# Splitting the fourth row group of the last convolution pass into three and two tiles, and moving the counts of the first search among the sums

## The reference, cut to what matters

```
m   = segment_sum(xt[src], dst) * Binv          # passes 0 and 2 (counts)
out = segment_sum(m[dst], src) * Dinv + b       # passes 1 and 3 (counts transposed)
h = prelu(hconv(x, W1, b1)); h = hconv(h, W2, b2) + x; x = x + prelu(h)
weights = layernorm(x) @ wr + br                # router
sel = the 1561 rows with the largest weights    # top-k
x[sel] += gelu(ln(x)[sel] @ w1 + b1) @ w2 + b2, times the weight of the row
```

## Time and profile before

| | |
|---|---|
| median of three runs | 1784.41 us |
| the three runs | 1784.41, 1785.26, 1777.81 us |
| the profiled execution | 1781.41 us |
| its span in the trace | 1779.7 us |
| PE busy | 1597.2 us (90%), 11957 matmuls |
| DVE busy | 1070.2 us (60%) |
| ACT busy | 1090.4 us (61%) |
| mean granted PE clock | 0.953 of full |

### The profile page before, as it was taken

The page is one execution under the profiler, slowest core; times in us unless marked ns, Lnnn a source line. Parts: engine busy times, 40 slices in busy tenths (PEclk is TensorE's granted clock), DMA queues, the critical chain, the costliest instruction groups (busy, mean ns, idle before and its releaser), DMA issues. The chain is left out here.

```text
span 1779.7 us, 35628 instructions
## 1 busy us (share of the span) xinstructions
PE 1597.2 (90%) x11957; PEld 1405.4 (79%) x11957; DVE 1070.2 (60%) x1890; ACT 1090.4 (61%) x1999; POOL 80.9 (5%) x116
## 2 busy tenths in 40 slices
PE   5777677699999999998999799999999999998697
PEld 4666666599999999996666599987789998776465
DVE  5598889579999999997455411214241122577671
ACT  2377778688888888884334466565665555565121
POOL 3000000000000000002000100000000000021213
PEclk9888888699999999998999899999999999999699
DMA  7325555256031212203000144445554444575211
GB/s 204 91 70 159 159 166 155 86 145 134 16 87 26 70 48 57 54 1 87 1 0 0 41 125 122 123 110 136 136 128 124 123 123 108 139 181 139 62 31 52
DMA packets 134299, 170.02 MB, mean 96 GB/s; under 512 B 17104, under 2 KB 125829, under 8 KB 134178
## 3 DMA queue, kind: packets, MB, share of 16 engines
q1 hardware_dynamic: 124268, 155.61, 33.3%
q0 software_dynamic: 6368, 9.36, 2.1%
q10 hardware_dynamic: 3542, 3.46, 0.8%
HBM read 114.58 MB, written 53.76 MB: 95 GB/s over the span
## 5 line engine op out<-in xcount | busy, mean ns | idle before, releaser
L1611 PE MATMUL ps_sets<-arena,kinds_mem 125*125 125x195 bf16 (+1 forms) x2500 | 447.4, 247 | 24.8 <-DVE kinds_mem L1370 16.7
L1354 ACT ACTIVATE kinds_mem<-ed_rows,es_mask 125x625 bf16<-125x625 f32 x500 | 367.2, 810 | 59.6 <-PE ps_sets L1617 31.3
L1617 PE MATMUL ps_sets<-arena,kinds_mem 125*125 125x195 bf16 (+1 forms) x2300 | 397.0, 248 | 0.0
L1611 PEld LDWEIGHTS ps_sets<-arena,kinds_mem 125*125 125x125 bf16 x2500 | 342.6, 137 | 31.8 <-DVE kinds_mem L1370 23.6
L2779 ACT ACTIVATE onewide<-ring 125x625 fp32r (+1 forms) x350 | 239.7, 721 | 180.4 <-PE oneps L2508 106.7
L1617 PEld LDWEIGHTS ps_sets<-arena,kinds_mem 125*125 125x125 bf16 x2300 | 308.3, 134 | 0.0
L2480 PE MATMUL oneps<-onewide,parts_a 125*128 125x376 f32 (+1 forms) x2000 | 294.3, 309 | 9.4 <-DVEq L2567 7.7
L2480 PEld LDWEIGHTS oneps<-onewide,parts_a 125*128 125x128 f32 x2000 | 292.3, 190 | 10.5 <-DVEq L2565 8.1
L2508 PE MATMUL oneps<-oneparts_b,onewide 125*125 125x512 f32 x1125 | 263.7, 395 | 0.0
L2508 PEld LDWEIGHTS oneps<-oneparts_b,onewide 125*125 125x125 f32 x1125 | 207.6, 185 | 54.7 <-DVE onefull L2639 2.1
L1362 DVE TENSOR_TENSOR kinds_mem<-kinds_mem,blk 125x2500 bf16<-125x2500 bf16 x120 | 182.4, 1520 | 33.9 <-ACT kinds_mem L1354 28.6
(11 more groups left out here) (457 smaller groups left out, 1838.5 us busy)
## 6 DMA issues: line engine op xcount, KB each, us to landing
ring<-counts SPq DMA_DIRECT2D x50, 683.6 KB
ring<-countsT SPq DMA_DIRECT2D x45, 683.6 KB
countsT<-kinds_mem SPq DMA_DIRECT2D x25, 683.6 KB
blk<-counts SPq DMA_DIRECT2D x20, 546.9 KB
counts<-blk SPq DMA_DIRECT2D x3, 3418.0 KB
counts<-kinds_mem SPq DMA_DIRECT2D x2, 3418.0 KB
ed_rows<-ed_dram SPq DMA_DIRECT2D x16, 273.4 KB
ring<-counts SPq DMA_DIRECT2D x50, 79.3 KB
```

The lines of the kernel that those rows point to most:

```text
L1354: return k.nc.scalar.activation(kinds_of(k)[:, slot, 0, :], k.ed_b[:, h, :], ACT.Relu, scale=MASK_SCALE, bias=k.es_mask[:, t, h:h + 1])
L1611: t_.matmul(out[0], kind[0], z[0], start=(t == 0), stop=False)
L1617: last = t_.matmul(out[1], kind[1], z[1], start=False, stop=(t == T - 1))
```

## The change

The fourth row group (i = 3) of pass 3 is taken out of the loops over the groups and is done as the last one is: tiles 0, 1, 2 over all t, then tiles 3, 4. Its chunks of counts are fetched twice as often, 125 x 375 and then 125 x 250 elements a t. DVE takes its banks part by part, finishes the rows of a part and does the dot products of that part at once; `x_done` is posted behind the rows of the second part, ahead of their dot products, and `row_weights` is cut into `row_dots` and `row_scales`. ACT takes the roots of group 2 ahead of t = 20 of group 3's first part, and those of group 3 ahead of t = 15 of group 4's first part. All eight counts of the search stand among the sums of the last group, the first at t = 14 of its first part instead of t = 20.

```diff
-def row_weights(dve, root_done, n, v, k, std, i, junk):
-    tiles = slice(i * U, (i + 1) * U)
+def row_dots(v, k, i, junk, some=range(U)):
+    tiles = slice(i * U + some[0], i * U + some[-1] + 1)
     v.tensor_copy(k.stat[:, tiles, 0], k.MV[:, tiles, 0])
     v.drain()
-    for u in range(U):
+    for u in some:
         t = i * U + u
         v.scalar_tensor_tensor(out=junk[:, u, :], in0=k.X[:, t, :], scalar=k.stat[:, t, 0:1], in1=k.wr_b[:, :],
                                op0=ALU.subtract, op1=ALU.mult, accum_out=k.dot[:, t:t + 1])
+    v.drain()
+
+def row_scales(dve, root_done, n, v, k, std, i):
+    tiles = slice(i * U, (i + 1) * U)
     dve.wait_ge(root_done, n)
     v.reciprocal(k.stat[:, tiles, 1], std[:, tiles])
...
-    COUNTS_AT = ((0, 20), (0, 24), (1, 5), (1, 10), (1, 15), (1, 20)) if len(counts) == 1 else ()
+    COUNTS_AT = ((0, 14), (0, 18), (0, 22), (0, 24), (1, 5), (1, 11), (1, 17), (1, 22)) if len(counts) == 1 else ()
+    def chunk_of(i, part):
+        return Q_LAST - 1 + (i - U + 2) * len(LAST) + part
...
-                for part in range(len(LAST)):
-                    for s in range(NS):
-                        last_counts_in(part, s)
+                for i in range(U - 2, U):
+                    for part in range(len(LAST)):
+                        for s in range(NS):
+                            last_counts_in(i, part, s)
...
-                            if (part, t) in COUNTS_AT:
+                            if i == U - 1 and (part, t) in COUNTS_AT:
                                 choice_counts(pe, t_, k, s1, COUNTS_AT.index((part, t)))
...
-                    with pe.Fori(1, U if c == 0 else U - 1) as i:
+                    with pe.Fori(1, U if c == 0 else U - 2) as i:
                         sums(2 * c + 1, i, {})
                 pe.wait_ge(z_free, 3 * 2 * U + 3)
-                last_sums()
+                last_sums(U - 2)
+                last_sums(U - 1)
...
-                def rows_out(n, i):
-                    v.tensor_scalar(tmp[:, :, :], full[:, :, :], 0.0, slope[:, 0:1], ALU.min, ALU.mult)
+                def rows_out(n, i, some=range(U)):
+                    part = slice(some[0], some[-1] + 1)
+                    v.tensor_scalar(tmp[:, part, :], full[:, part, :], 0.0, slope[:, 0:1], ALU.min, ALU.mult)
...
-                    means_out(3, i)
-                    rows_out(3, i)
-                    v.nop().then_inc(x_done, 1)
+                    for some in LAST if i == U - 2 else (range(U),):
+                        means_out(3, i, some)
+                        rows_out(3, i, some)
+                        if i == U - 2:
+                            if some[-1] == U - 1:
+                                v.nop().then_inc(x_done, 1)
+                            row_dots(v, k, i, full, some)
+                    if i < U - 2:
+                        v.nop().then_inc(x_done, 1)
...
-                weights(U - 2)
+                row_scales(dve, root_done, U - 1, v, k, std, U - 2)
+                v.nop().then_inc(weights_done, 1)
...
-                for i in range(1, U - 1):
+                for i in range(1, U - 2):
                     widen(3, i, {3 * U + 2: lambda: roots(i - 1)})
-                for part, some in enumerate(LAST):
-                    c0, c1 = some[0] * P, (some[-1] + 1) * P
-                    for t in range(TB):
-                        s = t // U
-                        if part == 0 and t == 3 * U + 4:
-                            roots(U - 2)
...
+                for i, root_at in ((U - 2, 4 * U), (U - 1, 3 * U)):
+                    for part, some in enumerate(LAST):
+                        c0, c1 = some[0] * P, (some[-1] + 1) * P
+                        chunk = chunk_of(i, part)
+                        for t in range(TB):
+                            s = t // U
+                            if part == 0 and t == root_at:
+                                roots(i - 1)
...
```

More of the change, by code:

```diff
@@ L2333, in convolutions_phase, with sums_before @@
     Q_LAST = 4 * U - 1
-    COUNTS_AT = ((0, 20), (0, 24), (1, 5), (1, 10), (1, 15), (1, 20)) if len(counts) == 1 else ()
+    COUNTS_AT = ((0, 14), (0, 18), (0, 22), (0, 24), (1, 5), (1, 11), (1, 17), (1, 22)) if len(counts) == 1 else ()
+    def chunk_of(i, part):
+        return Q_LAST - 1 + (i - U + 2) * len(LAST) + part
+    def sums_before(i):
+        return (U - 1) * (Q_LAST - 1) + (i - U + 2) * (U - len(LAST))
     with scope(nc, later) as (sb, pb, sem):
@@ L2385, in counts_in, with last_counts_in @@
                         sp.dma_start(ring[lo_:hi_, slot, :, :].rearrange("p a t d -> p (a t) d"), src[lo_:hi_]).then_inc(c_in[s % U], 16)
-                def last_counts_in(part, s):
+                def last_counts_in(i, part, s):
                     c0, c1 = LAST[part][0] * P, (LAST[part][-1] + 1) * P
-                    src = STEPS[3][s // U][(s % U) * QB:(s % U + 1) * QB, (U - 1) * QB + c0:(U - 1) * QB + c1].rearrange("(t p) d -> p t d", p=P)
-                    chunk = NS * (Q_LAST + part) + s
+                    src = STEPS[3][s // U][(s % U) * QB:(s % U + 1) * QB, i * QB + c0:i * QB + c1].rearrange("(t p) d -> p t d", p=P)
+                    chunk = NS * chunk_of(i, part) + s
                     sp.wait_ge(wide_done, U * chunk + U)
@@ L2514, in sums, with last_sums @@
                             after[s]()
-                def last_sums():
+                def last_sums(i):
                     for part, some in enumerate(LAST):
                         for t in range(TB):
-                            pe.wait_ge(wide_done, TB * (Q_LAST + part) + t + 1 + RB * U)
+                            pe.wait_ge(wide_done, TB * chunk_of(i, part) + t + 1 + RB * U)
                             for kk in some:
                                 if t == 0:
-                                    pe.wait_ge(c_out, U * Q_LAST + kk + 1)
+                                    pe.wait_ge(c_out, U * (3 * U + i) + kk + 1)
                                 last = t_.matmul(ps[0:P, kk, :], wide[:, t % RF, kk * P:(kk + 1) * P], ROWS[3][:, t % T, 0:2 * F],
@@ L2621, in means_out @@
                     for kk in some:
-                        if n == 3 and i == U - 1:
+                        if n == 3 and isinstance(i, int) and i >= U - 2:
                             part = LAST.index(tuple(some))
                             if kk == some[-1]:
-                                dve.wait_ge(wide_used, TB * (Q_LAST + part + 1) + RF)
+                                dve.wait_ge(wide_used, TB * (chunk_of(i, part) + 1) + RF)
                             else:
-                                dve.wait_ge(sum_done, (U - 1) * Q_LAST + kk - part + 1)
+                                dve.wait_ge(sum_done, sums_before(i) + kk - part + 1)
                         elif kk < U - 1:
@@ L2663, in residual @@
                     v.drain()
-                def rows_out(n, i):
-                    v.tensor_scalar(tmp[:, :, :], full[:, :, :], 0.0, slope[:, 0:1], ALU.min, ALU.mult)
+                def rows_out(n, i, some=range(U)):
+                    part = slice(some[0], some[-1] + 1)
+                    v.tensor_scalar(tmp[:, part, :], full[:, part, :], 0.0, slope[:, 0:1], ALU.min, ALU.mult)
                     v.drain()
-                    v.scalar_tensor_tensor(out=full[:, :, :], in0=full[:, :, :], scalar=0.0, in1=tmp[:, :, :], op0=ALU.max, op1=ALU.add)
+                    v.scalar_tensor_tensor(out=full[:, part, :], in0=full[:, part, :], scalar=0.0, in1=tmp[:, part, :], op0=ALU.max, op1=ALU.add)
                     v.drain()
                     if n == 3:
-                        rows = slice(i * U, (i + 1) * U)
-                        v.tensor_tensor(out=X[:, rows, :], in0=X[:, rows, :], in1=full[:, :, :], op=ALU.add)
+                        rows = slice(i * U + some[0], i * U + some[-1] + 1)
+                        v.tensor_tensor(out=X[:, rows, :], in0=X[:, rows, :], in1=full[:, part, :], op=ALU.add)
                         v.drain()
-                        for u in range(U):
+                        for u in some:
                             v.bn_stats(out=st[:, u, :], in_=X[:, i * U + u, :])
                         v.drain()
-                        for u in range(U):
+                        for u in some:
                             v.bn_aggr(out=mv[:, u, :], in_=st[:, u, :])
                         v.drain()
-                        v.tensor_copy(k.MV[:, rows, :], mv[:, :, :])
+                        v.tensor_copy(k.MV[:, rows, :], mv[:, part, :])
                         v.drain()
@@ L2696, in weights @@
                 def weights(i):
-                    row_weights(dve, root_done, i + 1, v, k, std, i, full)
+                    row_dots(v, k, i, full)
+                    row_scales(dve, root_done, i + 1, v, k, std, i)
                     v.nop().then_inc(weights_done, 1)
@@ L2794, in _ @@
                 widen(3, 0, {3 * U + 2: lambda: hi(2, U - 1)})
-                for i in range(1, U - 1):
```

(13 more changed lines are left out.)

6 lines of the change are left out of this document (3 added, 3 removed).

## The result

The changed kernel takes 1784.20 us (median of 20 runs, 1781.22 to 1788.62) against 1781.32 of the kernel before (20 runs): ratio 1.0018, 95% interval 1.0009 to 1.0026, that is 1.6 to 4.6 us slower. The profiled execution has 1784.62 us and a span of 1782.7, against 1781.41 and 1779.7.

The account below looks back on a forecast made before the run. Bound by DVE's chain of router weights, eight rounds and places, with PE as partner. Rounds +1.5 and clock +1.0 give +2.5 us: 1783.9 from the profiled execution, 1786.9 from the median, so 1785.4 predicted, range 1779 to 1791.

Parts of the forecast that it names:

- No change beyond 0.5%, +2.5 us: Whole kernel: +2.5 us in sum, within the 0.5% or 9 us a measurement can tell; same given 0.85.
- The start stays VectorE's: Start of group 3's finish: DVE still takes its banks at about 1608.8, though three banks are full about 12 us earlier.
- Extra VectorE work, net +1.1: Group 3's split on DVE: 1.9 us extra less 0.8 of waiting for roots; first counts ready at 1627.2, bounds +0.6 and +1.9.
- Stall of 3.9 us at (0, 14), first count 0.3 earlier, rounds 19.6: Last group: PE idles 3.9 us, first count at 1627.3, seven intervals 19.6 us against 17.85, eighth count +1.5 us.
- The clock, 1.0 taken from 0 to 1.7: Behind the new PE stall: a second dip to clock 0.50, costing 0 inside the stall, 1.7 fully behind it; 1.0 taken.
- ScalarE's wait is hidden: Last group's roots: ACT's own wait of 2.8 us costs nothing, as PE has five widened t in hand, then waits for the count.
- Group 3's chunks at no cost: Group 3's sums on PE, ACT and SP: 0 taken; late chunks, a rival of chance 0.07, would give about 1794.

Follow-up runs that it names:

- the move of the residual: Kernel before with group 4's residual done in VectorE's idle time ahead of group 2's banks, count places as before: ratio 0.9981, -3.4 us.
- the places alone: Kernel before with the eight new count places and nothing else, run twice: ratios 1.0011 and 1.0006 against before.
- the split as made: Changed kernel with the counts back at the six old places, group 3's roots still at t = 15: ratio 1.0013, +2.3 us against before.
- both moves and fitted places: Kernel before, group 3 undivided, group 4's residual and group 1's router weights moved ahead of group 2's banks, count places refitted, roots at t = 17: ratio 0.9963.
- The two split kernels with the moves: Changed kernel with that VectorE work moved, counts refitted, roots at t = 16: 0.9963; also with POOL's group 2 stores held until group 3 is finished: 0.9965.
- the split with late roots: Changed kernel with counts at the six old places and group 3's roots back at t = 19: ratio 0.9991, -1.6 us against before.
- the changed kernel with the stall filled: Changed kernel with 17 matmuls of 512 columns into an unused bank ahead of the first count: ratio 1.0006, +1.1 us against before.
- the whole kernel with later stores: Undivided kernel with the VectorE work moved, POOL's stores of group 2 held until group 3 is finished: ratio 0.9993, -1.2 us against before.
- the split kernel with the moves: Changed kernel with group 4's residual and group 1's router weights moved ahead of group 2's banks, counts refitted, roots at t = 16: ratio 0.9963.

## Why the prediction was right

1. *No change beyond 0.5%, +2.5 us.* Measured +3.2 (1.6 to 4.6) on the ratio, +2.93 in D. The forecast of 1785.4 us is only 1.2 above the 1784.20 measured because I had put the level between two values: with 20 runs the kernel before has 1781.32, the level of its profiled execution, and by that level the sum gives 1783.9.
2. *The start stays VectorE's.* Right: 1.22 us of idle TensorE before the last group, as the 1.33 of the earlier trace rows, and the move of the residual shows the cause.
3. *Extra VectorE work, net +1.1.* The first counts were ready 18.55 us behind the first bank, 17.31 before: +1.24. The halves of the wide instructions measured 0.96 + 0.69 against 1.49, as worked out from fixed parts: by these rows the fixed part is 0.16 us. I had set the rows against the 58 cycles, 0.06 us, of the Trainium skill, VectorE: DVE Perf Modes, "The TRN2 errata". I had read the table alone: below it the same section says that 58 is too low and gives 151 cycles at 0.96 GHz for an fp32 `tensor_tensor`, by an estimate 0.157 us, and the trace agrees.
4. *Stall of 3.9 us at (0, 14), first count 0.3 earlier, rounds 19.6.* Measured 4.19, 0.14 earlier, 19.43 with the clock held. But I saw the price in the places, and the places alone left D where it was: what they add to R (1.59) they take from C (1.42 to 1.75). The changed kernel pays because VectorE's extra 1.24 us takes back the gain in C.
5. *The clock, 1.0 taken from 0 to 1.7.* It was 1.5: the stretch at half speed, 1628.86 to 1632.28, began 0.6 us behind the first count at 1628.24 and lay wholly in the first interval. This is the term that was undersized. I had worked it out from a single dip; in other executions a like stall was followed by none, as the last section lists, so that it came is partly luck.
6. *ScalarE's wait is hidden.* Right in this kernel, 3.65 us with nothing lost; but by the stall alone. I had not said that it would cost 1.6 us without it.
7. *Group 3's chunks at no cost.* Right in price, wrong in the sign I gave for it: I named a wait for a DMA in group 3 as proof against me, and ScalarE waited 1.29 us. TensorE took 29.42 us for the group, 0.2 over 125 x 0.2335, and had 1.2 to spare. I judged by the 2.5 us landing of one chunk. By the rule of the Trainium skill, DMA: Bandwidth & Descriptors, Specifications, transfers under 512 B are below line rate. The waits of 1.29, 3.15 and 4.18 us were for chunks with 500-byte rows, but the longest, 5.02 us, was for one with 750-byte rows, so the rule does not explain them all; no run here isolates it.

The parts do not add up. By D the split as made costs 1.6 us at the old places and the places alone 0, together 2.9. Without the clock it is 1.45 together, near 1.6, but for another reason: at the old places the 1.6 are the early roots, which the stall hides in the changed kernel, and there it is VectorE's extra work that counts. The places gain 1.4 to 1.75 in C only while VectorE is early; the split takes that back, TensorE's stall is 4.2 instead of 2.6 us, and in the profiled execution the clock fell behind it.

## What to carry to other kernels

Count matmuls between the sync points of an in-order engine: a small matmul placed among long ones costs its partner the whole stretch between two of them, and a place too early costs the engine a stall. Fit the places to the partner's measured cycle. Before cutting a group in parts so that its finish can start early, see whether the finishing engine is free then; here moving 3.3 us of its work into an idle gap gave 3.4 us, and the cut without that moved D by 0.1, with its roots at the old t. With that work moved, the cut still gained nothing over the whole group. Cover is shared: a wait that is free because another wait hides it comes due when that one goes.

The kernel before with both moves and fitted places takes 1775.79 us (12 runs) against 1782.92 for the kernel before on the same chip: ratio 0.9963. It beats both kernels. The two split kernels with the moves, 0.9963 and 0.9965, are not told apart from it.

## What the runs showed of the hardware

*The clock behind short stalls of TensorE.* Like gaps were followed by half clock in one profiled execution and not in another. At the start of the last group TensorE is idle for about 2 us in three pieces: 2.2 us before and 1.9 in the changed kernel, both with a dip (the earlier trace rows and 1611.80 above), but 2.2 in the split with late roots and 1.6 in the changed kernel with the stall filled, both with none. Ahead of a count the stall of 4.19 us was followed by a dip, one of 2.64 us twice by none. Yet 1.63 and 2.30 us of waiting for widened counts, in the split and in the whole kernel with later stores, were each followed by a dip, and in the split kernel with the moves the clock fell within the 3.86 us ahead of the last group and stayed down for 6.83 us. In this order:

```profile
1632.52:1635.93 3.41, 3.41 (x9) 2.62 (x10) 1.17 (x7) 2.23 (x7) 0.00 (x0) 0.50 1.04 284
```

```profile
1636.73:1640.15 3.42, 3.42 (x10) 2.71 (x9) 1.61 (x7) 2.12 (x6) 0.00 (x0) 0.50 0.76 208
```

```profile
1607.42:1614.25 6.83, 4.88 (x12) 3.80 (x13) 5.66 (x17) 3.69 (x8) 0.00 (x0) 0.50 0.58 132
```

So in these traces the length of one stall does not decide it, and one profiled execution is no proof that a kernel has or lacks a dip.

*Idle time without a releaser.* VectorE sat idle for 0.43 us at L2693 of the changed kernel, shown above, and for 0.40 us ahead of the first counts' comparison in the kernel before (L2222). No run tells why. The two nearly cancel in item 3.
